# Priorities of the weight staging, and half of the gating multiplies moved from VectorE to GpSimd, in an eight-core transformer layer kernel

## The reference, cut to what matters

```python
x = x + attn(layernorm(x), ...)
x = x + ffn(layernorm(x), ...)

def attn(x):                      # x is 4 x 4096 x 1024 f32
    out = gelu(x)
    out_norm = out / norm(out)
    ema_sim = out_norm @ ema_norm
    seq_sim = max over earlier tokens s < t of out_norm[t] . out_norm[s]
    familiarity = w_seq * seq_sim + (1 - w_seq) * ema_sim
    gate = 1 - alpha + alpha * exp(-tau * familiarity)
    return out * gate

def ffn(x):
    gate = softmax(x @ gate_w.T)                  # 8 experts
    base = x @ weight.T                           # 1024 x 1024
    t = einsum('nh,erh->ner', x, lora_U)          # rank 16
    return base + einsum('ne,eor,ner->no', gate, lora_V, t) / 16
```

## Time and profile before

| | us |
|---|---|
| median of 2 runs | 412.77 (404.85 and 420.7) |
| the profiled execution, its own time | 403.61 |
| its span (slowest core, core 5) | 402.1 |
| spans of the 8 cores | 397.7 to 402.1 |
| mean granted TensorE clock of the cores | 0.934 to 0.935 |

### The profile page before, as it was taken

The page is one execution under the profiler, slowest core; times in us unless marked ns, Lnnn a source line. Parts: engine busy times, 40 slices in busy tenths (PEclk is TensorE's granted clock), DMA queues, the critical chain, the costliest instruction groups (busy, mean ns, idle before and its releaser), DMA issues.

```text
span 402.1 us, 5524 instructions; the slowest of 8 cores (397.7 to 402.1 us)
## 1 busy us (share of the span) xinstructions
PE 247.8 (62%) x1762; PEld 135.3 (34%) x1762; DVE 242.7 (60%) x537; ACT 129.4 (32%) x236; POOL 61.5 (15%) x38
## 2 busy tenths in 40 slices
PE   0000000027385878789498896989679887897791
PEld 0000000026243544445244443545344443443440
DVE  0291314447585857738624764469878996888723
ACT  1116000942957291731821173011212221222210
POOL 0000000078052415125013105100000000000000
PEclk9999999999886999989979999999889997998996
DMA  7732443017323232113303021223311222022222
GB/s 186 245 105 89 172 156 104 0 51 260 108 101 110 99 113 105 57 48 106 104 2 105 7 99 24 99 88 107 106 49 55 107 106 104 2 106 104 106 106 106
DMA packets 11665, 39.30 MB, mean 98 GB/s; under 512 B 1259, under 2 KB 2283, under 8 KB 11636
## 3 DMA queue, kind: packets, MB, share of 16 engines
q1 hardware_dynamic: 6528, 25.17, 17.8%
q10 hardware_dynamic: 5108, 13.78, 10.2%
HBM read 30.55 MB, written 8.39 MB: 97 GB/s over the span
## 4 chain that ended last, share of the span: by engine, by line
PE 34%; DVE 24%; issue 15%; ACT 13%; DMA 10%; DVEq 1%; POOL 0%; ACTq 0%; POOLq 0%; SPq 0%
PE ps L511 16%; PE ps L684 5%; PE ps L687 5%; DMA xbuf<-wt 4%; DVE st L415 4%; ACT xbuf L426 3%; ACT h L426 3%; PE ps L459 3%; DVE colbuf L532 3%; DVE st L414 2%; DMA identb<-ident 2%; PE ps L657 2%; DVE kT L465 2%; ACT L426 2%; PE ps L678 2%
## 5 line engine op out<-in xcount | busy, mean ns | idle before, releaser
L511 PE MATMUL ps<-kT 128*128 128x512 bf16 (+3 forms) x640 | 134.4, 363 | 20.1 <-DVE colbuf L532 6.6
L459 PE MATMUL ps<-identb,ktok 128*128 128x128 bf16 x256 | 21.9, 236 | 87.0 <-POOL ktok L450 64.8
L511 PEld LDWEIGHTS ps<-kT 128*128 128x128 bf16 x640 | 52.9, 101 | 66.6 <-issue 28.2
L532 DVE TENSOR_REDUCE colbuf<-ps 128x1 f32<-128x512 f32 (+3 forms) x80 | 47.4, 603 | 31.1 <-PE ps L518 16.5
L684 PE MATMUL ps<-wTb,kT 128*128 128x512 bf16 x128 | 51.4, 402 | 2.8 <-DVE mv L625 1.2
L450 POOL TENSOR_TENSOR ktok<-h,inv 128x1024 bf16<-128x1024 f32 x16 | 30.3, 1892 | 146.7 <-ACT inv L571 142.3
L687 PE MATMUL ps<-wTb,kT 128*128 128x512 bf16 x128 | 50.9, 398 | 0.0
L459 PEld LDWEIGHTS ps<-identb,ktok 128*128 128x128 bf16 x256 | 17.3, 106 | 90.2 <-issue 89.1
L469 ACT CAST kT<-ps 128x512 bf16<-128x512 f32 x32 | 18.5, 579 | 80.1 <-PE ps L459 73.5
L465 DVE CAST kT<-ps 128x512 bf16<-128x512 f32 x32 | 22.0, 687 | 28.5 <-PE ps L459 28.4
L450 POOL TENSOR_TENSOR ktok<-xbuf,inv 128x1024 bf16<-128x1024 f32 x16 | 31.3, 1954 | 49.9 <-PE ps L459 49.9
(11 more groups left out here) (98 smaller groups left out, 296.1 us busy)
## 6 DMA issues: line engine op xcount, KB each, us to landing
xbuf<-x SPq DMA_DIRECT2D x16, 1024.0 KB, 5.2
xbuf<-x ACTq DMA_DIRECT2D x8, 1024.0 KB, 5.1
y<-h SPq DMA_DIRECT2D x8, 1024.0 KB, 4.0
xbuf<-wt ACTq DMA_DIRECT2D x8, 512.0 KB, 4.4
xbuf<-ut ACTq DMA_DIRECT2D x1, 512.0 KB
xbuf<-vp ACTq DMA_DIRECT2D x1, 512.0 KB
xbuf<-gw ACTq DMA_DIRECT2D x1, 32.0 KB
identb<-ident ACTq DMA_DIRECT2D x1, 32.0 KB, 7.7
```

Source lines behind the costliest of these rows:

```text
L459: fns.append(lambda e, c=c, ps=ps: e.matmul(ps[:, (c % 4) * 128:(c % 4) * 128 + 128], ktok[:, buf, c * 128:(c + 1) * 128], ident[:, :], st ...
L511: fns.append(lambda e, c=c, pt=pts[bi], off=off, W=W, iswin=iswin: e.matmul(pt[:, 0:W], kT[:, c, 128 * m:128 * m + 128], kT[:, c, off:off ...
L532: p.op("vector", lambda e, pt=pts[bi], W=W, ci=cb_idx: e.reduce_max(colbuf[:, cbuf, ci:ci + 1], pt[:, 0:W], axis=AX), reads=[ptoks[bi]], w ...
```

## The change

The ten operations of the weight staging lose their `prio_bonus` of -150000, and all but the W loads and casts lose their stated cost too (they then count 150 ns in the plan). The reads of `("kT", ...)` that stood on the loads and on the W casts are gone. In `g_slot` the even slots stay as they were; in the odd slots two `tensor_tensor` operations on GpSimd take the place of one `scalar_tensor_tensor` on DVE, with `ztile` (one tile of f32, also the scratch of the sums of squares of partner tiles) between them.

```diff
     for c in range(NCHUNK):
         p.op("scalar", lambda e, c=c: e.dma_start(
             wstage[:, c % 2, :], wtd[c * 128:(c + 1) * 128, :]),
-            reads=[("kT", 2 * c, 0)],
-            writes=[("xbuf", c % 2)], dma=True, cost=2500.0, prio_bonus=-150000.0)
+            writes=[("xbuf", c % 2)], dma=True, cost=2500.0)
         p.op("vector", lambda e, c=c: e.tensor_copy(wTb[:, c, :], wstage[:, c % 2, :]),
-             reads=[("xbuf", c % 2), ("kT", 2 * c, 1)], writes=[("wTb",)],
-             cost=600.0, prio_bonus=-150000.0)
+             reads=[("xbuf", c % 2)], writes=[("wTb",)], cost=600.0)
     p.op("scalar", lambda e: e.dma_start(
         wstage[:, 0, :].rearrange("p (c j) -> p c j", c=8),
         utd.rearrange("(c q) j -> q c j", q=128)),
-        reads=[("kT", 15, 0)],
-        writes=[("xbuf", 0)], dma=True, cost=2500.0, prio_bonus=-150000.0)
+        writes=[("xbuf", 0)], dma=True)
     p.op("vector", lambda e: e.tensor_copy(
         uTb[:, :, :], wstage[:, 0, :].rearrange("p (c j) -> p c j", c=8)),
-        reads=[("xbuf", 0)], writes=[("uTb",)], cost=600.0, prio_bonus=-150000.0)
+        reads=[("xbuf", 0)], writes=[("uTb",)])
     p.op("scalar", lambda e: e.dma_start(wstage[:, 1, :], vpd),
-         reads=[("kT", 15, 1)],
-         writes=[("xbuf", 1)], dma=True, cost=2500.0, prio_bonus=-150000.0)
+         writes=[("xbuf", 1)], dma=True)
     p.op("vector", lambda e: e.tensor_scalar(vPb[:, :], wstage[:, 1, :], 0.0625, None, ALU.mult),
-         reads=[("xbuf", 1)], writes=[("vPb",)], cost=600.0, prio_bonus=-150000.0)
+         reads=[("xbuf", 1)], writes=[("vPb",)])
...
-        p.op("vector", lambda e, m=m, i=i: e.scalar_tensor_tensor(
-            h[:, m, :], h[:, m, :], gate16[:, m:m + 1], xbuf[:, i, :],
-            ALU.mult, ALU.add),
-            reads=[("h", m), ("gates", m // 4), ("xbuf", i)], writes=[("h", m)],
-            cost=1230.0)
+        if m % 2 == 0:
+            p.op("vector", lambda e, m=m, i=i: e.scalar_tensor_tensor(
+                h[:, m, :], h[:, m, :], gate16[:, m:m + 1], xbuf[:, i, :],
+                ALU.mult, ALU.add),
+                reads=[("h", m), ("gates", m // 4), ("xbuf", i)], writes=[("h", m)],
+                cost=1230.0)
+        else:
+            p.op("gpsimd", lambda e, m=m: e.tensor_tensor(
+                ztile[:, 0, :], h[:, m, :],
+                gate16[:, m:m + 1].broadcast_to([128, D]), ALU.mult),
+                reads=[("h", m), ("gates", m // 4)], writes=[("zt", 0)], cost=2300.0)
+            p.op("gpsimd", lambda e, m=m, i=i: e.tensor_tensor(
+                h[:, m, :], ztile[:, 0, :], xbuf[:, i, :], ALU.add),
+                reads=[("zt", 0), ("xbuf", i)], writes=[("h", m)], cost=2300.0)
```

## The result

| | before | after |
|---|---|---|
| median time, us | 404.99 (16 runs) | 406.69 (17 runs) |
| span of the profiled execution, slowest core | 402.1 | 404.2 |
| mean granted TensorE clock | 0.935 | 0.923 |

The ratio is 1.0044, 95% interval 1.0026 to 1.0062. I had forecast 388.6 us. The change costs a little; within 2% it makes no difference. So the gain at the start must have been given back somewhere, and the profile shows where.

A forecast was written before the change was run, and what follows sets the result against it. The prediction took the start as bound by latency around two staging slots and the last stage by a chain between PE and DVE, neither alone. It summed 403.6 - 15.0 (staging) - 0 (odd slots) = 388.6 us, range 378 to 398.

The forecast's parts named there:

- The loads and casts: Start: W loads and casts go ahead of statistics and group work, so the first-tile x load comes 15.0 us earlier.
- What was hidden in the old wait must find cover again: Start: the second group's gelus, at most 7.5 us, fit on ACT after the V load; otherwise up to 3 us go.
- The shift of 15.0 carries to the end: From the first x load on, everything shifts earlier by the same 15.0 us.
- I put the edit at 0.: Last stage: moving the odd slots to POOL nets about 0; bounds 10.2 us gained to 20 us lost.
- My own sign of being wrong: Wrong if x loads later than 52, or first gating operation to end (135 us) changes by more than 6 us.
- The add: Odd slots: the second POOL operation, reading two full tiles, was taken at 1.9 us, upper end 2.87.
- Meetings were counted by chance: Last stage: DVE and POOL operations taking turns cost 1.2 us per two slots, 9.5 over eight pairs.
- the saved 10.2 us: Last stage: DVE time freed by removing eight gating operations of 1.27 us each.
- The port decides the last stage: Rival, chance 0.06: each POOL operation stops DVE for its length, 20 us net, and PE's clock falls; 422 us.
- Its further 13.4 us from PE's lower clock: Last stage, part of the port rival: starved PE falls to its lower clock level in four more slots.
- DVE's relief counts in full: Rival, chance 0.14: in the last stage 8 of the 10.2 us freed on DVE are gained; 380.6 us.
- The total: Whole kernel: 403.6 us less 15.0 for the start and 0 for the odd slots, 388.6 us.

The follow-up runs named there:

- e5_soft: e1_staging with a planner rule letting other operations pass a weight-staging operation that heads a list but can't start yet; 392.3 us.
- e1_staging: The changed kernel with the odd slots' gating back on DVE, so the staging edit alone; 393.3 us.
- e2_pool: The kernel before with only the odd slots moved to POOL; 417.6 us.
- e3_shadow: e1_staging, DVE doing all 16 gating operations, plus 16 POOL operations of the same length whose result nobody reads; 405.9 us.
- e7_spread: e3_shadow with each added POOL pair released by its odd slot's normalization instead of the gate, reading only ztile and the gate; 400.2 us.
- e4_narrow: The changed kernel with every engine's list kept, but its 16 POOL operations only 8 elements wide; 392.9 us.
- e10_hnat: The kernel before with W, U and V staged in tiles of h instead of two shared slots, and without the low staging priorities; 374.1 us.

## Why the prediction was wrong

- *The loads and casts.* Right: W loads from 13.0, casts ahead of the statistics, W 7 ahead of U, x at 45.4 (forecast 46.1), first transpose at 70.4 (near 70).
- *"What was hidden in the old wait must find cover again ... They fit. If they do not, up to 3 us of the 15 go."* Wrong. I had allowed for gelus alone, between V and the new x. But I had myself used the rule that the first in rank blocks an engine's list, and it holds against the statistics too: each next cast is ranked first as soon as its load is planned, 2500 ns before it can run, so no statistic is placed between casts, and without statistics no gelu. What was lost is 5.7 us in the mean of the cores (first to ninth copy 35.6 for 29.9; 7 on the slowest cores), and the one rule of e5_soft gives it back (30.4).
- *The shift of 15.0 carries to the end.* e1_staging gained 11.5, and that it came this near is partly luck: 5.7 us of lost cover were set against some 3 us that a higher clock gave in the last stage, and neither was in the forecast. The rest after the ninth copy is 285 to 289 us (means) in all kernels without the POOL half and without a stall, and PE's clock took nothing back.
- *"I put the edit at 0."* The step that failed outright: it is +12.7 (e2_pool) or +12.5 (e3_shadow). My own sign of being wrong came with it: the stretch from the first gating operation to the end grew by 11.4 us, and I had allowed 6. Three of its terms were off. The add took 2.34 us where it met nobody, not 1.9:

```profile
L623 POOL TENSOR_TENSOR h<-ztile,xbuf x8: 2340/2580/3092, 260.1 to 342.8; 128x1024 f32<-128x1024 f32 x8
```

(the 2.25 us that I had estimated from the page GPSIMD Engine Reference of the Trainium skill, "Performance versus the Vector engine", was the better figure). Meetings were counted by chance, at a quarter of half an operation, 9.5 us; they were 13.6, because POOL's odd slot and DVE's even slot start at the same moment, within 0.11 us, in three of the four batches (2.87, 3.00 and 2.99 us at 258, 280 and 335); in e7_spread, where the gate no longer releases POOL, the gating operation lost 0.9 us. And I set the saved 10.2 us against them as if they were the same coin. By e4_narrow the relief, together with the new order, is worth 0.4 us. My reading, which no run isolates: DVE is full in parts of this stage, but what ends the slots is a chain through PE, DVE and ACT, and a hold of 1.6 to 2 us inside that chain delays it, while a shorter DVE leaves gaps.
- *The rivals.* "The port decides the last stage" had the mechanism and, with 20 us net from the meetings, the order of size; it was given 6%. Its further 13.4 us from PE's lower clock didn't come: the price is 10 to 12 us at a like clock (e3_shadow and e1_staging), and the busy time of PE grew by 5. "DVE's relief counts in full" falls by e4_narrow for the kernel as planned.
- *The total* of 388.6 was 18 us off: 12.5 from the meetings, 3.5 from the start (15.0 for 11.5), and 2 from setting out at 403.6 and not at 405.0 and from the rest.

## What to carry to other kernels

An operation moved from DVE to GpSimd has two prices that its duration doesn't show: DVE operations like the gating or the normalization here (two SBUF inputs, or a tensor_scalar from SBUF to SBUF) waited while such a GpSimd operation ran, and the two may be released by the same event. Ask first whether a shorter DVE would end anything sooner; a kernel that leaves the work out, with every list kept, tells it in one run. And when idle time is taken out of a start, list what ran inside it: here 5.7 of 13.6 us were cover for the next group, and a staging area that doesn't share slots with the first inputs (e10_hnat) was worth more than any order within two slots that was run. And compare all eight cores, not the two slowest: the first copy alone came 3 to 5 us apart between cores of one execution.

## What the runs showed of the hardware that was not expected

- A GpSimd memset of 128x1024 f32 takes 0.95 us and doesn't hold a two-input DVE operation (1270 ns, as alone), but does hold a one-source tensor_scalar (mean 896 for 804 ns, at most 1302).
- Even a DVE tensor_scalar of 8 elements is held: L712 rose from 231 to 380 ns in the mean, and to 1141 at most.
- A GpSimd tensor_tensor with a broadcast second operand takes 1.89 us for 128x1024 f32 whether it writes bf16 or f32; with two different full tiles it takes 2.34, and with the same tile as both operands (e7_spread) 1.89 again.
- With the same lists, PE's granted clock in the last stage differs between the cores of one execution (0.89 to 0.93 in e1_staging), and the stage takes 134.6 us at 0.89 and 130.4 at 0.93.
